# Which scores get the third PSUM bank: those of the exponentials in place of those of the maxima

## The reference

```
q, k, v = (einsum(xn, w) + b for each of the three)      # 16 heads of 8 channels
scores  = softmax(einsum('bhse,bhte->bhst', q, k) / sqrt(8))
att     = einsum('bhst,bhte->bhse', scores, v) -> (b, s, 128) @ wo.T + bo
ffn     = sigmoid(mix_r @ W_r.T) * (square(relu(mix_k @ W_k.T)) @ W_v.T)
out     = x + att + ffn
```

## Time and profile before

| | us |
|---|---|
| median of 3 runs | 483.36 |
| the 3 runs | 484.01, 479.1, 483.36 |
| the profiled execution: its own time | 477.82 |
| the profiled execution: span of its instructions | 476.0 |
| TensorE, busy in the span | 444.1 |
| VectorE | 402.4 |
| ScalarE | 393.3 |
| GpSimd | 367.9 |

### The profile page before, as it was taken

The page is one execution under the profiler, slowest core; times in us unless marked ns, Lnnn a source line. Parts: engine busy times, 40 slices in busy tenths (PEclk is TensorE's granted clock), DMA queues, the critical chain, the costliest instruction groups (busy, mean ns, idle before and its releaser), DMA issues. The chain is left out here.

```text
span 476.0 us, 15644 instructions
## 1 busy us (share of the span) xinstructions
PE 444.1 (93%) x5238; PEld 272.0 (57%) x5238; DVE 402.4 (85%) x823; ACT 393.3 (83%) x866; POOL 367.9 (77%) x675
## 2 busy tenths in 40 slices
PE   5698999999999999999999999999999999999994
PEld 4244656565656656565666566566655565666541
DVE  7488898888989998899999888899998889988920
ACT  2047988989888898989888889898898898988883
POOL 6577888888878898788888888788897888876321
PEclk8579999999999999999999999999999999999998
DMA  4444355454344544453455454344554443445100
GB/s 142 134 125 125 104 147 157 127 147 141 111 122 145 156 141 138 121 145 113 127 154 149 139 148 124 102 142 135 156 154 124 149 127 111 129 135 147 47 15 22
DMA packets 85836, 60.42 MB, mean 127 GB/s; under 512 B 6192, under 2 KB 73392, under 8 KB 85808
## 3 DMA queue, kind: packets, MB, share of 16 engines
q1 hardware_dynamic: 85808, 60.06, 44.1%
HBM read 29.89 MB, written 29.36 MB: 124 GB/s over the span
## 5 line engine op out<-in xcount | busy, mean ns | idle before, releaser
L524 DVE TENSOR_REDUCE neg_max<-bank_max 128x2 f32<-128x512 f32 x512 | 328.2, 684 | 44.6 <-PE bank_max L645 40.1
L425 ACT ACTIVATE probs<-bank_exp 128x512 f32<-128x512 f32 x512 | 278.7, 600 | 25.4 <-PE bank_exp L635 24.1
L635 PE MATMUL bank_exp<-ops 51*128 51x256 bf16 x1024 | 156.9, 272 | 4.1 <-issue 3.0
L645 PE MATMUL bank_max<-ops 48*128 48x256 bf16 x1024 | 159.2, 276 | 0.0
L584 PE MATMUL bank_val<-probs,val 128*25 128x256 f32 x2048 | 138.1, 383 | 1.2 <-ACT probs L425 1.2
L635 PEld LDWEIGHTS bank_exp<-ops 51*128 51x128 bf16 x1024 | 75.0, 94 | 77.0 <-issue 65.2
L584 PEld LDWEIGHTS bank_val<-probs,val 128*25 128x25 f32 x2048 | 55.8, 103 | 41.6 <-issue 20.2
L645 PEld LDWEIGHTS bank_max<-ops 48*128 48x128 bf16 x1024 | 76.4, 95 | 5.2
L335 POOL TENSOR_SCALAR xn<-x_in,moments,rstd 128x128 f32<-128x128 f32 x62 | 49.4, 804 | 0.0
L374 POOL TENSOR_TENSOR mixed_x<-mixed_x,xn_t 128x512 f32<-128x512 f32 x32 | 40.7, 1272 | 2.5
L386 POOL TENSOR_TENSOR y<-projected,rest 128x256 f32<-128x256 f32 x32 | 23.4, 732 | 21.7 <-ACT projected L458 21.7
(11 more groups left out here) (67 smaller groups left out, 635.1 us busy)
## 6 DMA issues: line engine op xcount, KB each, us to landing
ops<-spill SPq DMA_DIRECT2D x128, 192.0 KB, 3.4
spill<-qk_h SPq DMA_DIRECT2D x64, 192.0 KB, 3.3
spill<-qk_m SPq DMA_DIRECT2D x64, 128.0 KB, 2.0
x_in<-x SPq DMA_DIRECT2D x32, 128.0 KB, 2.2
spill<-qk_l SPq DMA_DIRECT2D x32, 128.0 KB, 1.8
y_out<-y SPq DMA_DIRECT2D x32, 128.0 KB, 1.9
ops<-shift SPq DMA_DIRECT2D x128, 6.0 KB
w<-weights SPq DMA_DIRECT2D x1, 448.0 KB, 3.2
```

Of the source, the lines that this page charges most:

```text
L425: nc.scalar.activation(probs[g % 2][:, u % G, :, :], bank_exp[u % 2][:, :, :], ACT.Exp, scale=SCALE).then_inc(exp_done[u], 1)
L524: nc.vector.tensor_reduce(out=neg_max[hf][:, :, r, pr], in_=bank_max[MAX_BANK[v]][:, :, :], axis=AX_X, op=ALU.max, negate=True).then_inc(m ...
L635: exp_mm = nc.tensor.matmul(bank_exp[r][:, i, :], ops[p][rows, hf, 1, pr, i * P:(i + 1) * P], ops[p][rows, hf, 0, pr, :], start=True, stop ...
L645: max_mm = nc.tensor.matmul(bank_max[MAX_BANK[v]][:, i, :], of[rows, max_hf, 0, max_pr, i * P:(i + 1) * P], of[rows, max_hf, 1, max_pr, :] ...
```

## The change

Three banks are given to the exponentials' scores and two to the maxima's. The bent rotation (now `EXP_BANK`) and the function that finds the unit before in the same bank go with the three banks, and the maxima alternate between two. No instruction is added, removed or moved; the two waits of each unit have other counts and semaphores.

```diff
-MAX_BANK = (0, 1, 2, 0, 1, 2, 0, 1, 0, 2, 1, 0, 2, 1, 0, 2)
+EXP_BANK = (0, 1, 2, 0, 1, 2, 0, 1, 0, 2, 1, 0, 2, 1, 0, 2)
...
-        bank_max = [psum(f"bank_max{i}", [P, ST, S]) for i in range(3)]
-        bank_exp = [psum(f"bank_exp{i}", [P, ST, S]) for i in range(2)]
+        bank_max = [psum(f"bank_max{i}", [P, ST, S]) for i in range(2)]
+        bank_exp = [psum(f"bank_exp{i}", [P, ST, S]) for i in range(3)]
...
 # ScalarE, unit u: reads bank_exp[EXP_BANK[u]] in place of bank_exp[u % 2]
 # VectorE, unit v: reads bank_max[v % 2] in place of bank_max[MAX_BANK[v]]
...
 # TensorE, ahead of the matmuls of unit u
-                        after(pe, exp_done[(u - 2) % H], n(0) if u >= 2 else n(-1))
+                        last_in_bank = before_in_bank(u)
+                        after(pe, exp_done[last_in_bank], n(0) if last_in_bank < u else n(-1))
...
-                        last_in_bank = before_in_bank(v)
-                        after(pe, max_done[last_in_bank], n(ahead) if last_in_bank < v else n(ahead - 1))
+                        after(pe, max_done[(v - 2) % H], n(ahead) if v >= 2 else n(ahead - 1))
...
-    nc.tensor.matmul(bank_exp[r][:, i, :], ...       # both kinds of scores, in the same places
+    nc.tensor.matmul(bank_exp[EXP_BANK[u]][:, i, :], ...
-    nc.tensor.matmul(bank_max[MAX_BANK[v]][:, i, :], ...
+    nc.tensor.matmul(bank_max[v % 2][:, i, :], ...
```

More of the change, by code:

```diff
@@ L50, with before_in_bank @@
 WARM = 9
-MAX_BANK = (0, 1, 2, 0, 1, 2, 0, 1, 0, 2, 1, 0, 2, 1, 0, 2)
-def before_in_bank(v):
-    return next(i for i in (*range(v - 1, -1, -1), *range(H - 1, v, -1)) if MAX_BANK[i] == MAX_BANK[v])
+EXP_BANK = (0, 1, 2, 0, 1, 2, 0, 1, 0, 2, 1, 0, 2, 1, 0, 2)
+def before_in_bank(u):
+    return next(i for i in (*range(u - 1, -1, -1), *range(H - 1, u, -1)) if EXP_BANK[i] == EXP_BANK[u])
 def rows_of(u):
@@ L424, in step @@
                             after(act, mix_psum[(g - 2) % NG], n(0) if g >= 2 else n(-1))
-                        nc.scalar.activation(probs[g % 2][:, u % G, :, :], bank_exp[u % 2][:, :, :], ACT.Exp,
+                        nc.scalar.activation(probs[g % 2][:, u % G, :, :], bank_exp[EXP_BANK[u]][:, :, :], ACT.Exp,
                                              scale=SCALE).then_inc(exp_done[u], 1)
@@ L523, in step @@
                             after(dve, max_split[hf], n(ahead - 1))
-                        nc.vector.tensor_reduce(out=neg_max[hf][:, :, r, pr], in_=bank_max[MAX_BANK[v]][:, :, :], axis=AX_X,
+                        nc.vector.tensor_reduce(out=neg_max[hf][:, :, r, pr], in_=bank_max[v % 2][:, :, :], axis=AX_X,
                                                 op=ALU.max, negate=True).then_inc(max_done[v], 1)
@@ L634, in step @@
                             rows = slice(RG * r, RG * r + KE)
-                            exp_mm = nc.tensor.matmul(bank_exp[r][:, i, :], ops[p][rows, hf, 1, pr, i * P:(i + 1) * P],
+                            exp_mm = nc.tensor.matmul(bank_exp[EXP_BANK[u]][:, i, :], ops[p][rows, hf, 1, pr, i * P:(i + 1) * P],
                                                       ops[p][rows, hf, 0, pr, :], start=True, stop=True)
@@ L639, in step @@
                             rows, of = slice(RG * r, RG * r + KS), ops[(p + ahead) % 2]
-                            nc.tensor.matmul(bank_exp[r][:, i, :], of[rows, max_hf, 0, max_pr, i * P:(i + 1) * P],
+                            nc.tensor.matmul(bank_exp[EXP_BANK[u]][:, i, :], of[rows, max_hf, 0, max_pr, i * P:(i + 1) * P],
                                              of[rows, max_hf, 1, max_pr, :], start=True, stop=True)
@@ L644, in step @@
                             rows, of = slice(RG * (1 - r), RG * (1 - r) + KS), ops[(p + ahead) % 2]
-                            max_mm = nc.tensor.matmul(bank_max[MAX_BANK[v]][:, i, :],
+                            max_mm = nc.tensor.matmul(bank_max[v % 2][:, i, :],
                                                       of[rows, max_hf, 0, max_pr, i * P:(i + 1) * P],
```

## The result

| | before | changed | ratio, 95% interval |
|---|---|---|---|
| first comparison, median of 4 and 4 | 481.6 us | 495.81 us | 1.029 (1.021 to 1.037) |
| second, on another occasion, median of 11 and 6 | 478.48 us | 496.44 us | 1.036 (1.034 to 1.039) |
| the profiled execution of each | 477.82 us | 497.13 us | (+19.3 us) |

The account below looks back on a forecast made before the run. TensorE was taken to set the pace, never waiting for a bank of scores. Losses of 13.0, 3.5, 2.0, 0.4 and 1.9 us less a 1.0 us gain gave +19.8 us, added to the 483.4 us median: 503 us (491 to 511).

Parts of the forecast that it names:

- unit 15: Unit 15 waits for the reduce two units before, 0.13 us in some 27 steps, a new loss of 3.5 us.
- The exponentials' side: Exponentials' bank distance goes from 2 to 3: nothing gained in the steady part, 1.0 us in step 31, at most 2.8.
- Unit 9: Unit 9, held by reduce 7, sets each step's loss: 0.42 us shared with units 5 and 7, 13.0 us over 31 steps.
- The lag: Delay from a reduce's end to the start of the TensorE unit waiting for it: 0.15 us, lower bound 0.06.
- Rival 3: At TensorE's waits for a reduce the short lag of 0.06 us holds: 13.2 us slower, 497 us; chance 14%.
- The first step of a loop turn: VectorE comes 0.40 us late, so unit 3 asks for 0.40 us more; five such steps, 2.0 us.
- Steps 29 and 30: In these two steps unit 9 asks for 0.60 us, 0.18 more than in others: 0.4 us together.
- Start: Steps -1 and 0, paced by VectorE: two banks lengthen the cycle of two reduces from 1.20 to 1.40 us; 1.9 us lost.
- Rival 1: TensorE has hidden room that takes in waits of 0.1 to 0.4 us: no change, 482 to 485 us; chance 7%.
- Rivals 2 and 4: 2: ScalarE paces TensorE, third bank frees it, 473 us, 5%; 4: every unit pays, 1.10 us a step, 517 us, 6%.
- TensorE's list of waits gets a new entry: Expected sign in the steady stretch: waits for VectorE's neg_max at units 9 and 15, some 15 us; L592's wait stays 9.7.
- never stops for a bank: Reading of the kernel before: steady-stretch TensorE waits are 9.7 us at L592 and 1.2 us issue, none for score banks.

Follow-up runs that it names:

- the waits without the banks: Kernel before with its own banks, but every unit waits for the reduce of two units before: 495.82 us against 479.0, ratio 1.036.
- the swap on TensorE alone: Kernel before with unit 1's weighted sums (L584) ahead of the transposes of L592 on TensorE, ScalarE's order kept: 473.72 us, ratio 0.990, the fastest version.

## Why the prediction was right, and where it was not

It said 503 us (491 to 511), slower by 4.1%; measured were 495.8 and 496.4, slower by 2.9% and 3.6%. The mechanism, TensorE held at unit 9 by VectorE's reduces, is confirmed. By stretches of the trace:

| us | forecast | measured |
|---|---|---|
| to the start of step 1: 1.9 and one step's 0.42 | 2.3 | 3.65 |
| steps 1 to 30: 12.6 + 3.5 + 2.0 + 0.4 | 18.5 | 15.30 |
| step 31 to the end | -1.0 | -1.30 |
| sum | 19.8 | 17.65 |

That the sum came so near is partly luck: one term was wrong (unit 15, 3.5 us), and others were too small.

- **"The exponentials' side: the gain in the steady part is nothing; 1.0 us in step 31."** Right: 0 and 1.3 us, by the kernel with two banks for either. The waits of weight loads for an Exp are gone from the list.
- **"Unit 9: 0.42 us a step."** Right: 0.43 us when it is put in alone, and unit 11 passes (0.23 us behind unit 10), as forecast. The account over units (0.05, 0.08, 0.29) was measured as 0.04, 0.07 and 0.28 us, by the spacing to the unit before (0.27, 0.30 and 0.51 us, in place of 0.23).
- **"The lag is 0.15."** Right, and its lower bound of 0.06 is the value for the wait that stands first. Rival 3, which took 0.06 for this order, falls; what the short lag is worth is measured by the swapped order, 0.11 us a step.
- **"Unit 15: a new loss of 0.13 us; the wait at L592 keeps its size and absorbs nothing."** Wrong, and this is the step of the sum that failed. The hold is there (0.13 us), but the chain behind it starts with ScalarE's Exps and not with TensorE's projection, and L592's wait gives it back: in the changed kernel that wait falls from 9.7 us to 6.7. The text followed the order of the code (projection, L410, L490, L592) and never compared when L410's data and when its engine were ready. That takes away 27 x 0.13 = 3.5 us, all but 0.02 a step.
- **"The first step of a loop turn: 0.40 us more."** Too small by a quarter: these steps went from 13.79 to 14.74 us, 0.50 more than the others gained. Steps 29 and 30 gained 0.66 and 0.76 us, where 0.60 were forecast. Against that, steps 2 and 7 of the kernel before are 0.56 and 0.81 us longer than its steady step, and those of the changed kernel are not, so 1.4 us of loss are missing there; the prediction didn't count these, and what makes them long stays open.
- **"Start: 1.9."** Step -1 bears it out: step 0 starts at 34.14 us in the second run of the changed kernel and at 34.17 in the kernel with two banks for either, before 32.00. Step 0 then takes 14.92 us in the one and 13.24 in the other, before 13.41, and the two have the same waits for a reduce. The third bank of the exponentials isn't the reason: with the waits without the banks, two for the exponentials, step 0 takes 14.70 us. What differs is the clock. Busy times from 36 to 41 us, in the kernel with two banks for either, then in the changed one (columns as in the earlier trace rows):

```profile
36.00:41.00 5.00, 4.58 (x52) 2.45 (x50) 4.36 (x9) 4.20 (x9) 3.79 (x8) 1.00 0.35 105
36.00:41.00 5.00, 4.92 (x38) 2.25 (x38) 2.98 (x6) 2.76 (x6) 3.11 (x7) 0.50 0.35 103
```

  With 1.2 in place of 2.4 GHz TensorE gets through 38 matmuls instead of 52. In the kernel before, the granted clock is 1.00 from 30 us on. Its mean from 15 to 60 us is 0.84 in the kernel before, with the wait at unit 15 alone, and with the swap on TensorE alone; it is 0.71 to 0.79 in the eight traces that have the new wait at unit 9. Two traces, the first of the changed kernel among them, have no clock on record that early and print 1.00; that one reaches step 1 at 49.87 us, and its score matmuls have rows of 0.39 us until 41 us and of 0.28 from then on. That the new waits cause the longer stretch at half clock fits this, but is not shown.
- **The sum and its base.** 19.8 us were forecast, 17.65 measured between traces. Adding the forecast to the median of three runs, 483.4, put it 5 us too high: the same kernel had a median of 478.5 in 11 later runs. The profiled execution's own 477.8 was the better base.
- **Rival 1 (hidden room).** Falls: 0.42 us of holding at unit 9 alone made the step 0.43 us longer. On that point the measurement decides against the Trainium skill's rule (Perfetto Trace Analysis, Identifying the Most-Contended Engine), which judges TensorE's headroom by weight-load time (and by the share of peak FLOPs, which was not worked out): weight loads fill 57 to 61% here, and in a steady step TensorE had no room but for one wait of 0.35 us. The rule's other half, that matmul busy time misleads, was borne out: it reads 369.3 and 369.1 of 380 us in the two kernels, though the second does 4% fewer matmuls.
- **Rivals 2 and 4.** No unit gained in the steady part, so 2 falls. 4 falls with the wait at unit 9 alone (0.43 of 0.45 us).
- **"TensorE's list of waits gets a new entry of some 15 us; L592's stays at 9.7."** Wrong twice: it got 1.0 us, for the list hides short holds, and L592 fell to 6.7. For the first reason "never stops for a bank" was argued too lightly from the earlier trace rows. It was true, but what shows it is the spacing of 0.23 us between units, not the list. The step went to 14.08 us, not 14.2, as the term of unit 15 fell away.

## What to carry to other kernels

When a buffer moves from one stream to another, list for each use how long before it the release comes, at the old and at the new distance: what counts is the worst use, here one unit of sixteen behind two extra VectorE operations, and not the mean load. Holds of the same chain don't add; they are counted again only from where the other engine waits in its turn. And before a delay is booked to the end of a chain, compare when the next instruction's data and when its engine are ready: the other of the two may be later already.

## What the runs showed of the hardware that was not expected

With two waits ahead of a matmul, the one that stands later in the code cost 0.147 us from the release to the start (units 5, 7, 9 and 15 of the changed kernel), and the earlier one 0.06 us (the reduce with the waits swapped, the Exp at unit 5 of the fastest version). The later one is waited for by an instruction of its own ahead of the weight load. Swapping them won 0.11 us a step, between 14.08 and 13.97.
